# Causal attention in a four-layer block: VectorE reduces both heads of a pair in one instruction where two neighbouring PSUM banks are free

## The reference

```
x = x + _L0_attn_a_ref(_layernorm(x, axis=-1), ...)      # gates f, i, o, s and a scan over the tokens
x = x + _L0_ffn_ref(_layernorm(x, axis=-1), ...)
x = x + _L0_attn_b_ref(_layernorm(x, axis=-1), ...)      # q, k, v; heads of 16 channels
x = x + _L0_ffn_ref(_layernorm(x, axis=-1), ...)

# inside the attention, for each head and each 64 queries:
scores = jnp.einsum('bhqd,bhkd->bhqk', qc, k) * scale
scores = jnp.where(causal_mask[None, None], -jnp.inf, scores)
m = jnp.max(scores, axis=-1, keepdims=True)
p = jax.nn.softmax(scores - m, axis=-1)
oc = jnp.einsum('bhqk,bhkd->bhqd', p, v)
```

## Time and profile before

| | |
|---|---|
| time, median of 3 runs | 1793.16 us (1791.85 to 1793.26) |
| profiled execution: its time / its span | 1792.9 us / 1791.2 us |
| PE, DVE, ACT, POOL busy | 96%, 87%, 73%, 30% of the span |
| granted TensorE clock | 0.993 of full speed |
| first reduction of a maximum starts, last one ends | 107.8 us, 1689.4 us |

### The profile page before, as it was taken

The page is one execution under the profiler, slowest core; times in us unless marked ns, Lnnn a source line. Parts: engine busy times, 40 slices in busy tenths (PEclk is TensorE's granted clock), DMA queues, the critical chain, the costliest instruction groups (busy, mean ns, idle before and its releaser), DMA issues.

```text
span 1791.2 us, 34351 instructions
## 1 busy us (share of the span) xinstructions
PE 1726.6 (96%) x12684; PEld 751.4 (42%) x12684; DVE 1553.3 (87%) x3102; ACT 1310.6 (73%) x2759; POOL 544.3 (30%) x841
## 2 busy tenths in 40 slices
PE   6799999999999999999999999999999999999997
PEld 5675555454444543344333453333433323333224
DVE  5778888889989999999998999999999999999702
ACT  2236576677687578866888758888788888888994
POOL 4336447534323722325221341321222101110001
PEclk9899999999999999999999999999999999999999
DMA  3132012002100310011000020000200000000000
GB/s 109 42 79 60 24 36 45 21 21 45 35 7 8 63 29 6 8 35 35 6 12 13 7 51 2 12 23 2 46 6 13 17 6 2 13 1 8 1 1 12
DMA packets 56955, 42.99 MB, mean 24 GB/s; under 512 B 8788, under 2 KB 56788, under 8 KB 56788
## 3 DMA queue, kind: packets, MB, share of 16 engines
q1 hardware_dynamic: 54548, 39.75, 9.2%
q10 hardware_dynamic: 2240, 1.05, 0.4%
HBM read 24.00 MB, written 16.25 MB: 22 GB/s over the span
## 4 chain that ended last, share of the span: by engine, by line
PE 34%; DVE 14%; ACT 5%; issue 1%; POOL 0%; DVEq 0%; POOLq 0%; ACTq 0%
DVE span_max L1308 13%; PE psum L1557 11%; PE psum L1536 7%; PE psum L1504 6%; PE psum L1371 4%; ACT probs L1078 4%; PE psum L1365 3%; PE psum L1359 1%; PE psum L1566 0%; PE psum L1511 0%; PE psum L1519 0%; DVE rows L1249 0%; DVE small L1167 0%; DVE rows L1301 0%; ACT oT L1085 0%
## 5 line engine op out<-in xcount | busy, mean ns | idle before, releaser
L1308 DVE TENSOR_REDUCE span_max<-psum 128x1 f32<-128x512 f32 (+3 forms) x2304 | 1312.8, 637 | 73.0 <-PE psum L1504 53.8
L1078 ACT ACTIVATE probs<-psum 128x512 f32<-128x512 f32 (+3 forms) x2304 | 1116.8, 573 | 203.0 <-PE psum L1536 200.0
L1557 PE MATMUL psum<-probs,v_aug 128*17 128x512 f32 (+3 forms) x4608 | 565.4, 562 | 2.8 <-POOL probs L967 2.0
L1504 PE MATMUL psum<-k_stack,q_stack 48*128 48x512 f16 (+3 forms) x2304 | 515.6, 362 | 7.3 <-DVE span_max L1308 5.1
L1536 PE MATMUL psum<-q_stack,k_stack 50*128 50x512 f16 (+3 forms) x2304 | 512.9, 365 | 4.4 <-ACT probs L1078 1.6
L1536 PEld LDWEIGHTS psum<-q_stack,k_stack 50*128 50x128 f16 x2304 | 138.9, 93 | 508.9 <-ACT probs L1078 439.5
L967 POOL TENSOR_SCALAR_AFFINE_SELECT probs<-probs 128x512 f32<-128x512 f32 x128 | 81.1, 636 | 566.6 <-ACT probs L1078 566.4
L1504 PEld LDWEIGHTS psum<-k_stack,q_stack 48*128 48x128 f16 x2304 | 166.8, 94 | 177.7 <-DVE span_max L1308 97.2
L1557 PEld LDWEIGHTS psum<-probs,v_aug 128*17 128x17 f32 x4608 | 76.5, 95 | 130.6 <-issue 112.5
L1004 ACT ACTIVATE rows<-psum,cols 128x256 f32<-128x256 f32 x128 | 53.7, 471 | 88.8 <-PE psum L1365 88.3
L1511 PE MATMUL psum<-mask_keys,mask_rows 64*128 64x64 bf16 x1024 | 91.5, 189 | 0.0
(11 more groups left out here) (122 smaller groups left out, 1412.2 us busy)
## 6 DMA issues: line engine op xcount, KB each, us to landing
q_stack<-q_parts SPq DMA_DIRECT2D x192, 32.0 KB, 2.0
k_stack<-k_parts SPq DMA_DIRECT2D x42, 128.0 KB, 4.6
rows<-in_x SPq DMA_DIRECT2D x16, 256.0 KB, 2.7
q_parts<-rows SPq DMA_DIRECT2D x32, 128.0 KB, 1.9
k_parts<-rows SPq DMA_DIRECT2D x32, 128.0 KB, 2.0
out<-rows SPq DMA_DIRECT2D x16, 256.0 KB, 2.2
x_rows<-rows SPq DMA_DIRECT2D x14, 256.0 KB, 2.2
rows<-x_rows SPq DMA_DIRECT2D x14, 256.0 KB, 2.7
```

What stands on the lines that cost most here:

```text
L1078: act.activation(probs[:, tile % PROBS, i, q0:], bank(b)[:, q0:], ACT.Exp, scale=SCALE / QK_SCALE).then_inc(exp_done, 1)
L1308: nc.vector.tensor_reduce(span_max[:, s % SPAN_RING, row:row + 1, k0 // SPAN:k0 // SPAN + 1], bank(b)[:, 0:k1 - k0], AX.X, ALU.max).then_i ...
L1504: ins = nc.tensor.matmul(bank(b)[:, 0:k1 - k0], q_stack[row:row + SCORE_ROWS, s % Q_RING, u, qt * P:(qt + 1) * P], k_stack[row:row + SCORE ...
L1557: ins = nc.tensor.matmul(pv_bank[32 * h:32 * h + VW, q0:], v_aug[:, j, g * HG + h, :], probs[:, tile % PROBS, h, q0:], start=(j == 0), sto ...
```

## The change

Four things change in the planner and one in the program.

1. When the planner has DVE take a reduction and the other half of the same piece lies in the neighbouring bank (half 0 in the lower one, half 1 in the upper) and is ready no more than `TOGETHER` later, it plans one operation `reduce2` for both. Both banks come free at its end.
2. `bank_for` is told the half. Among banks that are free equally early it prefers one whose neighbour on the right side is free too (`apart`), and for the second half the neighbour of the first (`beside`).
3. The numbers of the planner are others: `AHEAD`, `LEAD`, `TWO`, five entries of `WORTH`, and `MOST` now lets scores hold five banks.
4. The new operation waits for both halves' matmuls and reduces two rows of 512, 384, 256 or 128 columns, 2048 bytes apart, into two neighbouring rows of `span_max`.

```diff
-MOST = {"max": 4, "scores": 4, "job": 4}
+MOST = {"max": 4, "scores": 5, "job": 4}
...
-AHEAD = 18603
-LEAD = 13.5
-SOON, TWO = 0, -2100
+AHEAD = 37206
+LEAD = 14.5
+SOON, TWO = 0, -1800
+NEAR = -300
...
-WORTH = {"max": 2400, "dve": 1.0, "scores": 2650, "act": 1.562, "half": -2100, "pv": 2100, "stay": -6850,
-         "two": 1750, "ring": -5400, "last": -6600, "job": 1350, "age": 0.005, "same": 750, "after": -5250,
+WORTH = {"max": 2400, "dve": 1.0, "scores": 2650, "act": 1.562, "half": -2400, "pv": 2100, "stay": -7150,
+         "two": 550, "ring": -6000, "last": -6450, "job": 1350, "age": 0.005, "same": 750, "after": -5250,
...
+TOGETHER = 100
...
+    def apart(b, half, t):
+
+        other = b + (1, -1)[half] if half is not None else b
+        return half is not None and (beside is not None or not 0 <= other < BANKS or bank_free[other] > t + NEAR)
+
+    def bank_for(kind, t, half=None):
...
-        b = min(idle, key=lambda b: (max(bank_free[b], t), holder[b] != kind, b))
+        b = min(idle, key=lambda b: (max(bank_free[b], t), beside != b and apart(b, half, t), holder[b] != kind, b))
...
-                cost = 75 + (MAXIMA[k[1]][4] - MAXIMA[k[1]][3]) / 0.96
+                columns = MAXIMA[k[1]][4] - MAXIMA[k[1]][3]
+                cost = 75 + columns / 0.96
+                other = [o for o in ready["DVE"] if o[0] == "reduce" and o[1] == k[1]]
+                if other and other[0][3] - k[3] == other[0][2] - k[2] and ready["DVE"][other[0]] <= at + TOGETHER:
+                    at = max(at, ready["DVE"].pop(other[0]))
+                    cost = 75 + 2 * columns / 0.96
+                    k = ("reduce2", k[1], min(k[3], other[0][3]))
+                    name = "reduce2"
...
+            elif name == "reduce2":
+                bank_free[k[2]] = bank_free[k[2] + 1] = end
+                one_read(k[1], end)
                 one_read(k[1], end)
...
+                elif op[0] == "reduce2":
+                    _, m, b = op
+                    s, qt, u, k0, k1 = MAXIMA[m]
+                    row = qt * HG + u * 2
+                    for half in range(2):
+                        dve.wait_ge(m_full[half], m + 1)
+                    nc.vector.tensor_reduce(span_max[:, s % SPAN_RING, row:row + 2, k0 // SPAN],
+                                            psum[:, b * CHUNK:(b + 2) * CHUNK].rearrange(
+                                                "p (h k) -> p h k", h=2)[:, :, 0:k1 - k0],
+                                            AX.X, ALU.max).then_inc(span_reduced, 2)
```

More of the change, by code:

```diff
@@ L323, in schedule @@
     never = float("inf")
+    beside = None
     def width(tile):
@@ L327, in width @@
         return CHUNK - max(0, j - STEPS[s][1] * TT) * P
-    def bank_for(kind, t):
+    def apart(b, half, t):
+        other = b + (1, -1)[half] if half is not None else b
+        return half is not None and (beside is not None or not 0 <= other < BANKS or bank_free[other] > t + NEAR)
+    def bank_for(kind, t, half=None):
         taken = [b for b in range(BANKS) if bank_free[b] == never]
@@ L387, in on_pe @@
                 base = max(t, half_free[h]) if division == "half" else whole + SWITCH
-                can["max"] = (max(base, bank_for("max", t)[0], seen["load_q", s]), h)
+                can["max"] = (max(base, bank_for("max", t, h)[0], seen["load_q", s]), h)
         if scored < len(TILES) and ("place", TILES[scored][0]) in seen and scored < summed + PROBS:
@@ L486, in schedule @@
             s, qt, u, k0, k1 = MAXIMA[maxed]
-            b = bank_for("max", at)[1]
+            b = bank_for("max", at, how)[1]
+            beside = b + (1, -1)[how] if len(max_left) == 2 else None
             bank_free[b], holder[b] = never, "max"
```

## The result

The changed kernel takes 1800.04 us (median of 5 runs, 1798.76 to 1802.93) against 1793.16 us before in the same measurement: ratio 1.0042, 95% interval 1.0031 to 1.0053. It is slower by about 7.5 us by the ratio (the two medians differ by 6.9). The forecast was 1777 us, in a range of 1757 to 1797.

The account below looks back on a forecast made before the run. It took DVE as the bound in chunks 6 and 7, with PE as full as DVE in chunks 0 to 5. Terms -7.0 - 7.5 - 3.5 + 2.0 = -16.0 us on 1792.9 gave 1777 us, range 1757 to 1797.

Parts of the forecast that it names:

- Where the 21.9 us go: DVE's saving from 337 joined reductions: 7.0 us counted in full in chunks 6 and 7, 7.5 of 15.0 in chunks 0-5.
- the slower rival: Joined reductions free the first half's bank 0.53 us later, so PE waits: 1822 us; chance 0.15, shared with an unlucky order.
- the argument against the rival: Banks are given out with the longer hold entered, and a joined reduction is planned only where both banks are there.
- the second half is seldom late: DVE's joined reductions would seldom wait for PE's second half; 0 us counted.
- changes of manner: PE switches less often between half-array work, pv and jobs: 0.7 + 1.2 + 1.6 = 3.5 us less.
- the tail: Behind the last maximum, 154 score matmuls instead of 147 at ACT's pace: +3.4 us, net +2.0 us.
- how the waits fall: Effect of the planner's numbers through the new order's waits: nothing counted, 10 us either way in the range.
- the start-to-start row: Eighteen 512-column reductions in a row on DVE: 0.599 us from start to start, of which 65 ns is fixed part.
- The rival with the 50 us gain: On DVE each joining saves the whole 149 ns fixed part of the duration: 1742 us; chance 0.05 for the full 50 us.
- PE as the bound with nothing won from DVE: DVE's saving becomes idle time, leaving only -3.5 + 2.0: 1792 us; chance 0.18.

Follow-up runs that it names:

- the split: The changed kernel's order with each of the 337 joined reductions issued as two single ones, each releasing its own bank: 1799.04 us, ratio 1.0034.
- the old order joined: The kernel before, order kept and bank names exchanged, with 349 neighbouring pairs of reductions joined: 1880.55 us, ratio 1.0496.
- the single-reduction order with the fewest changes: The kernel before with AHEAD 37206, LEAD 14.5, five banks for scores and nearby worths, no joining: 1797.95 us, ratio 1.0031.
- the joined one with other numbers: Joining as in the change with LEAD 13.5, TWO -1500 and other worths, 347 joined reductions: 1803.38 us, ratio 1.0067.

## Why the prediction was wrong

**The step that failed** is *Where the 21.9 us go*: "Chunks 6 and 7: 107 x 0.065 = 7.0 us, which I count in full ... Between all (15.0) and nothing I take half, 7.5 us." That is 14.5 us of gain for joining. It measured, from the split to the changed kernel in one and the same order, 6.1 - 7.5 = -1.4 us, a loss or nothing. Three things are behind it, as the runs show:

- DVE's time is worth 0.29 of itself in the old order and 0.19 to 0.37 in the changed one, not 0.66 (14.5 of 21.9). A busy share of 97% did not make DVE the bound of chunks 6 and 7: the cut of 10.8 us there won 3.7 us, 0.34. PE's loads wait for both neighbours, 97.2 us for DVE and 439.5 us for ACT at the scores (with what PE computed meanwhile included), so a reduction that ends sooner helps only where DVE is the later one; that this is the reason is argued, not shown.
- Holding the first half's bank costs 2.7 us in the changed order, which is within the noise (the forecast's sum had nothing for it). I had this as the slower rival, with its place right. Its price I put at 0.13 us a pair (45 us for 337) and its condition at one pair in four; the old order pays 0.16 us a pair. But the change plans its order with the hold in it, and in that order the price is 0.01 us, as the argument against the rival had it; the longer time to the bank's next use (0.97 us in the median against 0.42) fits this.
- "By the earlier trace rows the second half is seldom late, so I take nothing for waiting for it." In the old order joined this was wrong: 34 us of the loss are this, all in the 130 pairs written apart. In the changed order it held: joined only where the halves are written together, the kernel takes the same time.

**The second term that was off** is the order itself. The prediction gave it -3.5 us for changes of manner, +2.0 us for the tail, and "nothing ... with 10 us either way" for how the waits fall. It measured +6.1 us (changed kernel, split). The tail came as forecast: 105.9 - 101.8 = 4.1 us longer, against 3.4. The term for changes of manner did not show as a gain: half-array work rose by 9.5 us with seven runs fewer, and the single-reduction order with the fewest changes is 5.6 us slower than before. The price of a change may be right, but it is small beside how the half-array work falls: this is 694.7, 699.9, 709.7 and 727.3 us in the four single-reduction orders made by the planner, and their times are 1789.0, 1792.6, 1798.0 and 1828.2 us, in the same sequence. Kernels with holds or joined reductions fit this only roughly: the joined one with other numbers has 707.9 us and takes 1803.4.

**What was right.** The number and the size: 65 ns a pair by the start-to-start row and not 149 by the duration. The joined form at 1219 ns for 1216. Less exact: DVE's busy time should have fallen by 22 us and fell by 12.8. The reductions alone (their union) fell by 18.9 us, from 1312.8 to 1293.9, and the durations of DVE's other 798 instructions add up to 5.1 us more than before (315.6 against 310.5). The rival with the 50 us gain is out. PE as the bound with nothing won from DVE (1792 us) was nearer than the forecast, but it is not what happened either: cutting DVE's work does win time.

**Sum as measured**: order +6.1, hold +2.7, joined instruction -1.3: +7.5 us. The last two are each within the noise; the first is not.

**What stays open.** Joining saves 22 us of DVE's time and wins 1.3 us, while 22.7 us cut out of the columns of the same reductions win 8.2. The two gains differ by 6.9 us, and the intervals of the three runs allow about 5 either way, so the difference is hardly more than noise. Idle time before the reductions does not explain it, for it grew alike in both. Second halves written late do not either: leaving out the 53 pairs written apart changed nothing (+6.6 against +7.5). A joined reduction begins later than the first of two single ones could, and leaving out columns moves no beginning; what that costs is not measured here. Why these two orders differ in their waits at all was not traced to single places; the runs show only that every change of the planner's numbers tried here brought such differences.

## What to carry to other kernels

When a planner writes the whole order, compare a change in two steps: the new order with the old instructions, and the new instruction in the old order. The first showed here that 6 of 7.5 us were the draw of an order, which no cost of an instruction explains. An instruction that reads two buffers releases both at its end and starts when both are full; with seven banks in turn the hold alone cost 0.15 us a pair, more than a saved fixed part of 65 ns, unless the order is made for it (0.01 us). And before counting a saving on an engine that is busy 97%, measure what its time is worth: cut some columns and see what share comes through (0.2 to 0.4 here). Cut them also as the control for a reading of idle time: what grows with any cut says nothing about the new instruction.

## What the runs showed of the hardware

A reduction over two neighbouring PSUM banks takes what its columns take, 1219 ns for 2 x 512, and 1.13 us from start to start in the median; there is no charge for the step between banks. Back to back, the fixed part of a reduction is 65 ns, though 149 ns stand in its duration.
